# Who writes the mask: four more heads a beat given from TensorE to ScalarE in a transformer's first attention

## What is computed

```python
def mha(q, k, v, wq, bq, wk, bk, wv, bv, wo, bo, mask):
    ...
    att = jnp.einsum('bhqd,bhkd->bhqk', Q, K)
    if mask is not None:
        att = jnp.where(mask == 0, jnp.float32(-1000000000.0), att)
    att = jax.nn.softmax(att, axis=-1)
    out = jnp.einsum('bhqk,bhkd->bhqd', att, V)
    ...
    return out @ wo + bo
x1 = mha(x, x, x, m1_wq, ..., tgt_mask)
x2 = layer_norm(x + x1, ln1_g, ln1_b)
x3 = mha(x2, enc_out, enc_out, m2_wq, ..., src_mask)
x4 = layer_norm(x2 + x3, ln2_g, ln2_b)
```

## Time and profile before

| | |
|---|---|
| median of the runs | 1344.96 us |
| the profiled execution's own time | 1344.11 us |
| its span, first to last instruction | 1342.4 us |
| mean granted clock of TensorE | 0.946 |
| beat 0 starts (exp of head 0) | 71.21 us |
| last exp of beat 15 | 419.54 us |
| a middle beat (8), mask of head 0 to the next | 253.94 to 276.51 us |

### The profile page before, as it was taken

One profiled execution on the slowest core, in us unless ns is written; L12 is line 12 of the kernel. 1 busy time (PEld: TensorE's weight loads), 2 busy tenths in 40 slices (PEclk: granted clock), 3 DMA queues, 4 the chain that ended last, 5 costly groups with the idle time before them and its releaser, 6 DMA issues. The chain is left out here.

```text
span 1342.4 us, 27195 instructions
## 1 busy us (share of the span) xinstructions
PE 1171.6 (87%) x8287; PEld 944.8 (70%) x8333; DVE 796.2 (59%) x3047; ACT 624.2 (47%) x1515; POOL 540.8 (40%) x866
## 2 busy tenths in 40 slices
PE   4689999999987999899999999446988877699996
PEld 3466667666654888789999999433656644689995
DVE  4588878888873388865333343176868965423231
ACT  2278787878885233143333333111655544233331
POOL 3334454545433254545333333231544533333331
PEclk9799999999999999899999999866999988799998
DMA  4766675545421971122222222167634884511110
GB/s 107 172 139 167 140 168 112 113 101 115 97 38 20 379 203 33 48 41 37 41 34 40 41 33 36 17 148 167 152 84 116 167 272 152 189 34 48 39 37 5
DMA packets 113526, 136.98 MB, mean 102 GB/s; under 512 B 23115, under 2 KB 99801, under 8 KB 108476
## 3 DMA queue, kind: packets, MB, share of 16 engines
q1 hardware_dynamic: 98152, 106.08, 33.1%
q0 software_dynamic: 15232, 29.17, 9.6%
HBM read 101.85 MB, written 35.97 MB: 103 GB/s over the span
## 5 line engine op out<-in xcount | busy, mean ns | idle before, releaser
L797 DVE CUSTOM_DVE_ANT_0 att_masked_scores<-att_S,Bm 128x256 bf16<-128x256 f32 x512 | 190.3, 418 | 38.2 <-PE att_S L539 26.9
L2459 ACT ACTIVATE moe_hT<-moe_H,moe_b 128x128 f32<-128x128 f32 x312 | 89.0, 368 | 171.5 <-PE moe_H L2372 171.0
L672 ACT ACTIVATE att_PT<-att_T 128x512 f32<-128x512 f32 x256 | 146.2, 591 | 47.6 <-PE att_T L561 43.6
L2384 PE MATMUL moe_Z<-moe_W,moe_hT 128*128 x624 | 141.6, 380 | 0.8 <-DVE moe_z L2684 0.8
L2384 PEld LDWEIGHTS moe_Z<-moe_W,moe_hT 128*128 128x128 f32 x624 | 115.5, 190 | 15.5 <-issue 1.2
L2547 POOL DMA_INDIRECT x<-Y,X x39 | 63.6, 1632 | 154.7 <-DVE Y L2695 150.8
L539 PE MATMUL att_S<-L_KS,L_QS 96*128 96x256 bf16 x512 | 99.3, 276 | 20.3 <-DMA L_KS<-att_k_dram 13.8
L561 PE MATMUL att_T<-L_QS,L_KS 99*128 99x256 bf16 x512 | 97.4, 272 | 11.2 <-ACT att_T L677 3.7
L1825 DVE TENSOR_REDUCE out_mx<-out_S 128x2 f32<-128x512 f32 x128 | 85.4, 685 | 34.5 <-PE out_S L1257 33.4
L2684 DVE TENSOR_TENSOR moe_z<-moe_Z,moe_b 128x256 f32<-128x256 f32 x39 | 16.6, 424 | 141.9 <-PE moe_Z L2384 141.9
L2372 PEld LDWEIGHTS moe_H<-moe_aT,ff_w 128*128 128x128 f32 x832 | 96.8, 192 | 3.1 <-issue 1.9
(11 more groups left out here) (469 smaller groups left out, 2524.2 us busy)
## 6 DMA issues: line engine op xcount, KB each, us to landing
moe_W<-in_L_ffn_W SPq DMA_DIRECT2D x16, 1024.0 KB, 13.7
L_W<-in_L_ffn_W POOLq DMA_DIRECT2D x12, 1024.0 KB, 10.5
att_q_dram<-att_pq SPq DMA_DIRECT2D x16, 384.0 KB, 4.4
att_k_dram<-att_pk SPq DMA_DIRECT2D x16, 384.0 KB, 2.8
L_QS<-att_q_dram SPq DMA_DIRECT2D x16, 384.0 KB, 4.9
L_KS<-att_k_dram SPq DMA_DIRECT2D x16, 384.0 KB, 8.1
L_QS<-att_q_dram SPq DMA_DIRECT2D x16, 256.0 KB, 5.7
L_KS<-att_k_dram SPq DMA_DIRECT2D x16, 256.0 KB, 8.7
```

What stands on the lines that cost most here:

```text
L672: nc.scalar.activation(PT[:, h % 8, :], bankT[h % 2][:, :], ACT.Exp).then_inc(exp_done, 1)
L797: ins = nc.vector.tensor_tensor_reduce(masked_scores[:, h % 2, u, :], bankS[h % 2][:, u * SEQ:(u + 1) * SEQ], masks[m // B][0][:, u * SEQ: ...
L2384: ins = nc.tensor.matmul(bankZ[:, 0:D], eT[:, s % 2, f * P:(f + 1) * P], w2e[:, f, :], start=(f == 0), stop=(f == NF - 1))
L2459: ins = nc.scalar.activation(eT[:, s % 2, g * P:(g + 1) * P], bankH[half][:, f * P:(f + 1) * P], ACT.Relu, bias=b1[:, bass.ds(e * NF + g, 1)])
```

## The change

ScalarE's mask write is used for four even heads of each unit as well: heads 10, 12 and 14, and head 0 of the next unit (not of the first). It stands right behind the exps of heads 8, 10, 12 and 14, so from head 8 on every exp is followed by a mask write; at heads 0 to 7 only the odd ones are, as before. For the late heads TensorE issues no identity matmul and waits for a semaphore of their own, `late_seeded`. Nothing else is changed.

```diff
-        seeded = sem("seeded")
+        seeded, late_seeded = sem("seeded"), sem("late_seeded")
...
+        late = lambda m, h: h % 2 == 0 and (h >= H // 2 + 2 or h == 0 and m >= 1)
+        late_no = lambda m, h: 4 * m + max(h - H // 2, 0) // 2
...
                 dst = bankT[h % 2]
-                if h % 2 and (m, h) != (0, 1):
+                on_mask = h % 2 and (m, h) != (0, 1) or late(m, h)
+                if late(m, h):
+                    pe.wait_ge(late_seeded, late_no(m, h))
+                elif on_mask:
                     pe.wait_ge(seeded, seed_no(m, h))
                 else:
                     pe.wait_ge(exp_done, H * m + h + 1)
...
-                                           skip_group_check=h % 2 == 1 and (m, h) != (0, 1))
+                                           skip_group_check=bool(on_mask))
...
-                nc.scalar.activation(bankT[1][:, :], masks[layer][1][:, :], ACT.Copy).then_inc(seeded, 1)
+                nc.scalar.activation(bankT[h % 2][:, :], masks[layer][1][:, :], ACT.Copy).then_inc(seeded if h % 2 else late_seeded, 1)
...
-                        if h % 2 and (b, h) != (M - 1, H - 1):
+                        if (h % 2 or h >= H // 2) and (b, h) not in ((M - 1, H - 1), (M - 1, H - 2)):
                             seed(b, h)
```

## The result

The changed kernel takes 1355.11 us (median of 6 runs, 1352.09 to 1358.14) against 1345.59 of before: ratio 1.0067, 95% interval 1.0046 to 1.0088, or 9.0 us (6.2 to 11.8). The two medians lie 9.5 us apart. The direction, the place and the range (1342 to 1360) were right; 6 us were forecast.

What follows compares the result with a forecast made beforehand. TensorE seemed to set the pace, with ScalarE the bound in half a beat after the change. Terms 0.86 - 0.28 + 2.04 + 0.45 + 0.59 + 1.42 + 0.85 = 5.9; 1344.96 + 6 = 1351 us, range 1342 to 1360.

Steps and rivals of the forecast that it cites:

- The sign and the cause in the large: First attention: slower, because ScalarE's solid chain from head 8 to head 0 eats TensorE's relief of 0.88 us a beat.
- The middle beats: Beats 6 to 11: each 0.34 us longer, 2.04 us in all.
- the walk: Head-by-head timing of beat 8 with the new writes, from exp 8 to the next head 0, then applied to other beats.
- The first-order rule for a late head: Late heads' scores start 0.66 us after the start of the mask write; their exp follows 0.42 later.
- Beat 0: No output projection and so no idle to fill: next head 0 released at 93.02 for 92.16, 0.86 us longer.
- Beats 1 to 3: Beats 1 and 2, half as late: 0; beat 3, with TensorE waiting for a transfer at head 8: 0.14 us earlier.
- Beats 4 and 5: Beat 4: 0.34 us longer, going under in beat 5's wait for keys; beat 5's walk ends 0.14 earlier.
- Beat 12: No rows to turn but a longer wait for its projection: 0.45 us longer.
- Beats 13 to 15: No query, key or value projections, so ScalarE sets the pace throughout: 0.59, 1.42 and 0.85 us longer.
- Rival 1: TensorE's relief comes through: 63 x 0.22 = 13.9 us faster, 1331 us; chance 0.12.
- Rival 2: ScalarE becomes the bound of whole beats: 28 us slower, 1373 us; chance 0.15 for more than 10 us.
- Rival 3: Steady beats don't change, only beat 0 and the last ones: 3 us slower, 1348 us; chance 0.2.

Runs made afterwards that it cites:

- unmasked: Changed kernel with no mask at all for the late heads, neither TensorE matmul nor ScalarE write: middle beat 22.37 us, ratio to before 0.9988.
- act_8_10: Kernel before plus two ScalarE writes a beat, behind the exps of heads 8 and 10, into a buffer nobody reads: middle beat 23.05 us for 22.56.
- rows_first: Changed kernel, but at head 10 ScalarE copies the turned rows before writing the mask for head 12: middle beat 23.31 us for 23.16.
- only0: Changed kernel with only the next head 0 late, one write a beat behind the exp of head 14: middle beat 22.82 us, against 22.56 before.
- late14_mq: Changed kernel with only head 14 late and VectorE's small negated-maxima steps moved behind head 8's maxima: middle beat 22.19 us, ratio to before 0.9967.
- before_mq: Kernel before with VectorE's two small negated-maxima steps moved from behind head 7's maxima to behind head 8's: middle beat 22.41 us, ratio 0.9992.

## Why the prediction was right, and where not

- **The sign and the cause in the large.** Confirmed. The moved masks free 0.88 us a beat on an engine that gains little by it here (0.19 in `unmasked`), and lengthen ScalarE's row between the exps of heads 8 and 0, whose one long idle is filled. The exps of head 8 to head 0 took 10.52 us for 10.4 forecast, the idle before head 13 is down to 0.10 and the one before head 1 is left.
- **The middle beats**, 0.34 forecast, 0.60 measured: the mis-sized term, 6 x 0.26 = 1.6 us, and the same in beat 4. The step that failed is "head 12 needs the mask of 270.98 [...] The projection behind it carries that on". It lists the copy of the turned rows at 271.52, and so its end at 272.1, but has the projection start without it. `act_8_10` and `rows_first` show that the projection waits for this copy through the shared bank; where TensorE keeps its identity matmuls, that alone makes a beat 0.44 to 0.49 longer. The wait for the mask at head 12, on which I had put the price, was there but covered by it.
- **How the 0.60 comes together** can be read from the starts, against the exp of head 1 of beat 8 (256.75 before, 261.46 after). In the changed kernel the scores of head 13 are 0.55 late. Head 14 gets its 0.22 back, and its exp, released by its scores (280.24 to 280.67), is 0.34 late, where the walk had 0.16. From there to the scores of the next head 0 it takes 1.37 (to 282.04) where it took 1.11 (the rows of the kernel before are below): 0.26 more, as much as head 0 alone costs in `only0`. So it is 0.34 behind the projection and 0.26 for the wait at the next head 0. Of the 0.26 that the walk lacks, 0.18 is the projection. The rest, some 0.09, is in the last wait: from the write to the scores it took 0.75, not 0.66.

```profile
275.62 1.09 ACT L672 ACTIVATE att_PT<-att_T 128x512 f32<-128x512 f32 x2
```
```profile
276.73 0.38 PE L561 MATMUL att_T<-L_QS,L_KS 99*128 99x256 bf16 x2
```

- **The first-order rule for a late head**, write to release 0.66 us, release to exp 0.42: right at heads 11 and 12 (275.64 to 276.29 is 0.65). At the next head 0 it is 0.75 (281.29 to 282.04), in `only0` as well. The prediction had allowed 0.1 more for TensorE's load and fill; whether that is the cause no run shows.
- **Beat 0**: 0.86 forecast and measured. **Beats 1 to 3**: 0, 0 and -0.14 forecast, 0.26, 0.07 and 0.38 measured. **Beats 4 and 5**: 0.61 in beat 4, of which 0.41 goes under in beat 5's wait for the keys, as said. **Beat 12**: 0.77 for 0.45.
- **Beats 13 to 15**: 2.86 forecast, -0.27 + 1.32 + 0.74 = 1.79 measured. Beats 14 and 15 are within 0.11. In beat 13 TensorE waits for keys, 1.4 us in place of 2.2, so the heads behind it are less late than the walk has it; the walk had not let a transfer swallow anything there. Beat 13 takes 18.5 to 20.0 us over all these kernels, so one profile each doesn't fix its share.
- **The sum**: 5.9 forecast, 7.95 in the trace, 9.0 (6.2 to 11.8) timed. That it came so near is in part luck: beats 1 to 12 are 3.1 us above the walk and beats 13 to 15 are 1.1 below. The delay went through the barrier: the next stage starts 9.8 us later, 1.7 of it the slow clock at the start of this one profile; the rest of the kernel took 910.5 us for 912.4, which is within what these profiles scatter (906.6 to 913.7).
- **Rival 1**, relief comes through: out. Even without any price (`unmasked`) only 0.19 of 0.88 us a beat comes through, because of VectorE, which the walk leaves out. Part of that is VectorE's collision with GpSimd: without it, the relief of head 14 comes through in full (`late14_mq`).
- **Rival 2**, ScalarE as the bound of whole beats: out, its idle before head 1 is 1.06 us. The rule of the Trainium skill that stood beside it (Perfetto Trace Analysis, Identifying the Most-Contended Engine) pointed the right way here, but gives no size: ScalarE's 43 us of new work cost 9.
- **Rival 3**, the middle beats don't change: out, they are 0.60 longer.

## What to carry to other kernels

Before moving work to an engine "with room", find its longest stretch without idle between two points where it meets the bottleneck, and walk the moved instruction through that stretch; a share of 85% busy alone does not tell it. In the walk, every instruction that gets later must be asked what it frees (here a bank that another task shares), not only what it computes. Put such work into an idle that ends in a wait for the bottleneck: the same write that cost 0.26 us at one head was free at another.

## What the runs showed of the hardware

A VectorE instruction on 32 columns with two inputs in SBUF took 0.19 us or 1.18 us, depending on whether a GpSimd instruction of 1.16 us had started just ahead of it. Both kinds occur within one execution, where the two starts lie within 0.01 us of each other. One such collision a beat cost 0.15 us in the kernel before and 0.40 with head 14 late, and it is hard to see, since the long instruction counts as VectorE's busy time.

TensorE's granted clock was 0.51 in a window of 5 us at the start of the stage in `after` and 1.00 there in the kernel before. In windows of 4 us behind the keys' wait it was 0.62 in `before_mq` (wait of 4.0 us) and 0.57 in `late14_mq` (1.9 us), but 1.00 in the kernels before and after (2.4 and 3.0 us). The length of that wait alone doesn't order them. A comparison of single profiles has to look at the clock of each stretch first.
